# Graph network kernel: key one-hots as steps made by one Sign, counts from halved differences of neighbouring columns

## The reference

```python
x_j = x[src]
v_j = x_j[:, :384].reshape(E, 128, 3)
s_j = silu(x_j[:, 384:] @ W1 + b1) @ W3 + b3
edge_basis = rbf(edge_attr2) * cutoff @ W2 + b2
s1, s2, s3 = split(s_j * edge_basis)
v_msg = v_j * s1[:, :, None] + s3[:, :, None] * edge_attr1[:, None, :]
x = x + segment_sum(concat([v_msg, s2]), dst)
# second round: a message depends on the sender's node alone
msg2 = f(x, U, V, Wu1, Wu2)
x = x + segment_sum(msg2[src], dst)
out = layernorm(x_in + x)
```

## Time and profile before

| | |
|---|---|
| median of 3 runs | 541.85 us (537.26 to 544.62) |
| profiled execution | 537.99 us, of which the span is 536.1 us |
| PE busy | 461.1 us (86%), 5180 matmuls |
| DVE busy | 450.7 us (84%), 767 operations |
| ACT busy | 442.5 us (83%), 836 operations |
| POOL busy | 362.2 us (68%), 395 operations |

### The profile page before, as it was taken

The page is one execution under the profiler, slowest core; times in us unless marked ns, Lnnn a source line. Parts: engine busy times, 40 slices in busy tenths (PEclk is TensorE's granted clock), DMA queues, the critical chain, the costliest instruction groups (busy, mean ns, idle before and its releaser), DMA issues.

```text
span 536.1 us, 14464 instructions
## 1 busy us (share of the span) xinstructions
PE 461.1 (86%) x5180; PEld 291.1 (54%) x5181; DVE 450.7 (84%) x767; ACT 442.5 (83%) x836; POOL 362.2 (68%) x395
## 2 busy tenths in 40 slices
PE   4782989888997999997989899898899899789995
PEld 3321445455654655564655565565565566468784
DVE  4587899899999999999998999999999998641192
ACT  2362999888998999899899999999999999586442
POOL 8854777777777777777777777777777777370100
PEclk9765799899999999999999999999999999979999
DMA  8945888888888888888888888888888888410022
GB/s 230 334 157 153 251 263 261 261 274 269 261 246 280 258 273 272 258 253 268 264 254 262 284 264 261 270 269 260 238 259 266 279 274 263 153 45 1 2 99 98
DMA packets 46625, 123.17 MB, mean 230 GB/s; under 512 B 9379, under 2 KB 22249, under 8 KB 46545
## 3 DMA queue, kind: packets, MB, share of 16 engines
q0 software_dynamic: 25120, 102.91, 62.1%
q1 hardware_dynamic: 16993, 13.13, 7.9%
q10 hardware_dynamic: 4432, 6.10, 3.5%
HBM read 110.11 MB, written 12.00 MB: 228 GB/s over the span
## 4 chain that ended last, share of the span: by engine, by line
PE 29%; DVE 17%; POOL 17%; issue 13%; DMA 12%; ACT 11%; ACTq 1%; DVEq 1%; SPq 0%; POOLq 0%
POOL side L590 11%; PE psum L1512 8%; DMA side<-node_table,src_c 6%; DVE side L1091 5%; POOL work L590 5%; PE psum L1369 4%; PE psum L1407 4%; ACT side L714 4%; DMA xw<-in_x 3%; ACT scratch L723 3%; PE psum L1401 3%; PE psum L1381 2%; DVE side L1088 2%; DMA work<-node_table,src_c 2%; PE psum L1362 1%
## 5 line engine op out<-in xcount | busy, mean ns | idle before, releaser
L590 POOL DMA_INDIRECT side<-node_table,src_c x234 | 236.2, 1009 | 71.3 <-issue 67.7
L714 ACT ACTIVATE side<-key_no,less_key 128x320 bf16<-128x320 f32 x314 | 160.6, 567 | 0.4
L723 ACT ACTIVATE scratch<-side,one_f 128x640 bf16<-128x640 bf16 x157 | 129.6, 825 | 0.0
L1401 PE MATMUL psum<-side,scratch 128*32 128x512 f32 x468 | 124.0, 609 | 0.3 <-DVE side L1091 0.3
L1091 DVE TENSOR_TENSOR side<-side,psum 128x768 f32<-128x768 f32 x117 | 110.7, 946 | 0.0
L590 POOL DMA_INDIRECT work<-node_table,src_c x80 | 82.5, 1032 | 36.3 <-issue 34.5
L1369 PE MATMUL psum<-w2s,scratch 128*128 128x384 bf16 x314 | 79.2, 335 | 29.8 <-DVE side L1091 23.6
L1407 PE MATMUL psum<-side,scratch 128*32 128x128 f32 x1404 | 99.1, 277 | 0.0
L1088 DVE TENSOR_TENSOR side<-side,psum 128x512 f32<-128x512 f32 x117 | 79.6, 680 | 12.0 <-DMA side<-node_table,src_c 11.5
L1407 PEld LDWEIGHTS psum<-side,scratch 128*32 128x32 f32 x1404 | 71.6, 110 | 0.1
L1381 PE MATMUL psum<-scratch 128*128 128x320 bf16 x314 | 65.6, 318 | 0.0
(11 more groups left out here) (227 smaller groups left out, 772.1 us busy)
## 6 DMA issues: line engine op xcount, KB each, us to landing
side<-node_table,src_c POOLq DMA_INDIRECT x234
sum_rows<-stage SPq DMA_DIRECT2D x208, 16.0 KB
sum_rows<-zeros_bf SPq DMA_DIRECT2D x1, 2688.0 KB, 19.3
node_table<-work ACTq DMA_DIRECT2D x8, 320.0 KB, 2.9
scratch<-sum_rows SPq DMA_DIRECT2D x10, 256.0 KB, 4.6
out<-xw SPq DMA_DIRECT2D x9, 256.0 KB
xw<-in_x ACTq DMA_DIRECT2D x1, 1728.0 KB
work<-node_table,src_c POOLq DMA_INDIRECT x80
```

Of the source, the lines that this page charges most:

```text
L590: g.indirect_dma_start(out=rows[i % SLOT_PAIRS][:, j, :], out_offset=None, in_=node_table, in_offset=bass.IndirectOffsetOnAxis(ap=src_c[:, ...
L714: a.activation(key_off[:, b, j, :], key_no[:, :], ACT.Abs, bias=less_key[:, t:t + 1]).then_inc(L["key_off_made"], 1)
L723: a.activation(key_hot[:, n % 2, t:t + 2, :], key_off[:, b, :, :], ACT.Relu, bias=one_f[:, :], scale=-1.0).then_inc(L["key_hot_made"], 1)
L1401: mm(bank[b][j * SPAN:(j + 1) * SPAN, :], hot[:, n % 2, t + j, 0, :], rows[s][:, j, 0:4 * C], start=first, stop=True, skip_group_check=True)
```

## The change

The key one-hot of an edge becomes a step. `key_no` gets 33 columns a window in place of 32 (STEPS = SPAN + 1, KEYS = 330) and holds the column's key less one half. Sign(key_no + less_key) is -1 for columns up to the edge's key and +1 beyond it. One ACT operation a tile writes it straight into `key_hot`; the buffer `key_off` and its Relu go. PE multiplies as before, on 330 columns. Half the difference of two neighbouring columns of the product is the count of the one-hot. `add_counts` therefore takes two operations: `part_sum` = 0.5 x columns 1 to 32 + `counts`, then `counts` = -0.5 x columns 0 to 31 + `part_sum`, with a wait of DVE on its own first operation between. In the setup, the iota of `key_no` grows to 330 columns and its copy becomes a tensor_scalar.

```diff
-    KEYS = NW * SPAN
+    STEPS = SPAN + 1
+    KEYS = NW * STEPS
...
-        key_off = r_side.cut(4 * KEYS, BF16).rearrange("p (b j k) -> p b j k", b=2, j=2)
+        part_sum = r_side.cut(NW * SPAN).rearrange("p (s d) -> p s d", s=NW)
...
-            g.tensor_copy(key_no[:, :], key_no_i).then_inc(S["pool_const"], 1)
+            g.tensor_scalar(key_no[:, :], key_no_i, 0.5, None, ALU.add).then_inc(S["pool_const"], 1)
...
-            def key_offsets(i):
-                b = i % 2
-                if i >= 2:
-                    act.wait_ge(L["key_hot_made"], i - 1)
-                for j in range(2):
-                    t = 2 * i + j
-                    a.activation(key_off[:, b, j, :], key_no[:, :], ACT.Abs, bias=less_key[:, t:t + 1]
-                                 ).then_inc(L["key_off_made"], 1)
-
             def key_hots(i):
-                n, b = group_of(i), i % 2
+                n = group_of(i)
                 t = 2 * (i - GP * n)
-                act.wait_ge(L["key_off_made"], 2 * i + 2)
                 if n >= 2:
                     act.wait_ge(L["counted"], n - 1)
-                a.activation(key_hot[:, n % 2, t:t + 2, :], key_off[:, b, :, :], ACT.Relu, bias=one_f[:, :], scale=-1.0
-                             ).then_inc(L["key_hot_made"], 1)
+                for j in range(2):
+                    a.activation(key_hot[:, n % 2, t + j, :], key_no[:, :], ACT.Sign, bias=less_key[:, 2 * i + j:2 * i + j + 1]
+                                 ).then_inc(L["key_hot_made"], 1)
...
                 for i in range(PAIRS):
                     if i + GP < PAIRS:
-                        key_offsets(i + GP)
-                    if i + GP - 1 < PAIRS:
-                        key_hots(i + GP - 1)
+                        key_hots(i + GP)
...
-                v.tensor_tensor(into, into, bank[6][:, 0:KEYS].rearrange("p (s d) -> p s d", s=NW), ALU.add
-                                ).then_inc(L["counts_taken"], 1)
+                sums = bank[6][:, 0:KEYS].rearrange("p (s d) -> p s d", s=NW)
+                v.scalar_tensor_tensor(out=part_sum, in0=sums[:, :, 1:STEPS], scalar=0.5, in1=into, op0=ALU.mult, op1=ALU.add
+                                       ).then_inc(L["half_added"], 1)
+                dve.wait_ge(L["half_added"], n + 1)
+                v.scalar_tensor_tensor(out=into, in0=sums[:, :, 0:SPAN], scalar=-0.5, in1=part_sum, op0=ALU.mult, op1=ALU.add
+                                       ).then_inc(L["counts_taken"], 1)
...
-                pe.wait_ge(L["key_hot_made"], GP * n + tiles.stop // 2)
+                pe.wait_ge(L["key_hot_made"], 2 * GP * n + tiles.stop)
```

More of the change, by code:

```diff
@@ L37 @@
 MARGIN = 500
-SCRATCH = 20736
-SIDE = 9328
+SCRATCH = 20800
+SIDE = 9264
 HIGH_AT = 256
@@ L279, in build @@
         sums_in = [sem(f"sums_in{b}") for b in range(2)]
-        loop_names = """products_made basis_made src_hot_made key_off_made key_hot_made hot_made counted summed
+        loop_names = """products_made basis_made src_hot_made key_hot_made hot_made counted half_added summed
         copied combined sums_taken counts_taken table_step stored start_in angle_made turn_near turn_made sin_made wave_made
@@ L448, in _ @@
                     sp.wait_ge(L["src_hot_made"], LG)
-                    sp.wait_ge(L["key_off_made"], 2 * PAIRS)
-                    sp.wait_ge(L["key_hot_made"], PAIRS)
+                    sp.wait_ge(L["key_hot_made"], 2 * PAIRS)
+                    sp.wait_ge(L["half_added"], LG)
                     sp.wait_ge(L["hot_made"], 2 * LG)
@@ L534, in _ @@
             g.iota(lane_i, pattern=[[0, 1]], base=0, channel_multiplier=1).then_inc(S["pool_const"], 1)
-            g.iota(key_no_i.rearrange("p (s d) -> p s d", s=NW), pattern=[[KEY_STEP, NW], [1, SPAN]], base=0,
+            g.iota(key_no_i.rearrange("p (s d) -> p s d", s=NW), pattern=[[KEY_STEP, NW], [1, STEPS]], base=-1,
                    channel_multiplier=0).then_inc(S["pool_const"], 1)
@@ L788, in key_pass @@
                 for i in range(GP):
-                    key_offsets(i)
-                    if i:
-                        key_hots(i - 1)
+                    key_hots(i)
                 for i in range(PAIRS):
                     if i + GP < PAIRS:
-                        key_offsets(i + GP)
-                    if i + GP - 1 < PAIRS:
-                        key_hots(i + GP - 1)
+                        key_hots(i + GP)
                     if i % 2 and (i + 5) // 2 < QUADS:
@@ L1255, in _ @@
                 with dve.Fori(0, EXTRA) as r:
-                    dve.wait_ge(L["key_off_made"], 2 * PAIRS)
+                    dve.wait_ge(L["key_hot_made"], 2 * PAIRS)
                     dve.wait_ge(L["sums_taken"], LG)
```

## The result

The changed kernel takes 546.89 us in the median of four runs (545.35 to 550.14), the kernel before 539.56 us (535.91 to 544.62, four runs as well). The ratio is 1.0145 with a 95% interval of 1.0103 to 1.0187: slower, by more than nothing and by less than 2%. The profiled execution took 547.02 us with a span of 545.2 us, against 537.99 and 536.1 us. The forecast was 548 us.

A forecast was written before the change was run, and what follows sets the result against it. POOL's gathers were taken to pace the kernel, DVE next behind. DVE's 27.7 us of added work less 18.0 us of waits gave +9.7 us on the profiled 537.99 us: 548 us, range 542 to 555 us.

The forecast's parts named there:

- The pacer: In the pass, POOL's stream of gathers, 413 us, sets the pace, with DVE next behind at 95% busy.
- a round's 1.77 us less 0.95 us: ACT's one-hots: two Sign replace two Abs and a Relu, so ACT loses 0.8 us a pair, 129 us in 157 pairs.
- the later `key_hots`: In ACT's queue, `key_hots` of a new group runs later, behind `counted`, and still fits: cost 0.
- 1 to 3 us on the counts: On PE, 314 count matmuls grow from 320 to 330 columns: 1 to 3 us, hidden behind DVE, cost 0.
- The term a group: DVE's addition: two operations of 495 ns, the second waiting for the first, add 544 ns a group.
- by the rule: Between DVE's two additions, a semaphore costs nothing extra: a group would add 413 ns, giving +3.4 us, 541 us.
- rival B: DVE's second operation overlaps freely, or the usual execution leaves DVE more idle time: 541 to 544 us, chance 0.22.
- The waits: DVE's waits in the pass for gathered rows and ACT, 18.0 us together, vanish as DVE becomes late.
- rival C: DVE's waits move instead of vanishing, as later `counts_taken` holds PE's next count: 557 to 566 us, chance 0.18.
- Rival D: Faster: ACT was the real pacer and DVE's operations hide; gathers shrink, 518 us at best, chance 0.03.
- 27.7 - 18.0 = +9.7 us: In the pass, 27.7 us more DVE work less 18.0 us of filled DVE waits leaves +9.7 us.
- it moves as a whole: Behind the last message, the chain of last adds, copy, store and read of sums shifts without growing.

The follow-up runs named there:

- The kernel with ACT unrelieved: Kernel before with its two Abs and Relu kept on ACT, but two dependent halved additions on DVE: 547.41 us, ratio 1.0128.
- Both experiments without DVE's waits: Kernel before with only the two halved additions on DVE, 547.41 us; changed kernel with its first addition done twice, 564.74 us.
- DVE's part alone: Kernel before with Abs and Relu kept on ACT and the sums added in two dependent halves on DVE: 547.41 us, ratio 1.0128.
- the one with three additions: Changed kernel with the first addition done twice, the copy going to a spare buffer: 564.74 us, ratio 1.0459.

## Why the prediction was right, point by point

**The pacer.** I read POOL as the pacer and DVE as next behind. The swap fits: the stream of gathers measures 413.18 us before and 413.60 after. POOL issued as before, and it was DVE that ended 5.3 us later. That DVE had 18.4 us to spare before, and has none now, is measured. That POOL, and nothing else, set the pace before is read from its unbroken stream; no run on a 540 us chip changed the stream, or took work from DVE, to test it. The reading left out that POOL also waits 1.8 us for slots at `work`, in 6 waits, none over 0.3 us. It changes nothing.

**ACT.** Forecast busy 315 us, measured 337.2. The Sign costs what the Abs cost (566 ns at 330 columns, 567 at 320), which I had. The error is in the subtraction. I took a round's 1.77 us less 0.95 us, and both are times from start to start with the next operation right behind. A pair of Abs is busy for 1.01 us, so that 0.76 us is nearer. It lost 0.67 us a pair (105.3 us by 157) and not 0.8. I put the remaining 0.09 us down to overlap that ACT's operations lose now that it stands idle between them, which wasn't measured by itself. I also priced the later `key_hots` as fitting. It did: ACT's 87.7 us at L715 are a wait for `counted` with slack behind it, and DVE never waits for ACT in the pass.

**PE.** Forecast 1 to 3 us on the counts, hidden. The row grew from 65.6 to 67.3 us.

**DVE's two operations.** Forecast 495 ns each with 0.034 us between, measured 481 and 493 ns with 0.034 us. The term a group was +0.544 us and measured +0.524 (26.70 us by 51), mostly because the first operation is 14 ns cheaper. The 413 ns a group that the prediction gives "by the rule" don't follow from my own 495 ns, by which it is 2 x 413 - 398 = 428 ns, the upper end of rival B. That changes neither B's range nor its chance. The rival B fell with its first half, a second operation that overlaps, as the timeline at 144.38 shows, and so did its 541 to 544 us. Its second half, more idle time in the usual execution, comes up under the size.

**The waits.** Forecast -18.0 us, measured -18.4. This was rival C's point: waits could move instead of vanishing. None moved into DVE's pass. Rival D, a faster kernel, fell with it: DVE was the bound as soon as its waits were used up.

**The step that failed: "27.7 - 18.0 = +9.7 us".** The two terms were right to 1 us, but a third was missing. The other operations of DVE took 3.0 us less. In the pass before, 32 operations outside the dependent pairs started without overlapping their forerunner (26 behind idle gaps, 6 behind gaps that are too short to count as idle). After, there is 1. Each of these starts loses the 0.08 us of overlap besides its wait. 31 x 0.08 = 2.5 us, most of the 3.0. The kernel with ACT unrelieved has nearly the same saving with 4 such gaps left (its other operations take 369.3 us, the changed kernel's 368.8, those of before 371.8), so it comes from DVE being late and not from ACT.

**The other step that failed: "it moves as a whole".** The tail grew by 3.2 us. The first 0.8 us lie at PE. Its timeline around the end of the last message (start us, us, instruction), before and then after, and DVE's addition of the last group after:

```profile
464.37 1.04 PE L1381 MATMUL psum<-scratch 128*128 128x320 bf16 x6
465.75 0.62 PE L1401 MATMUL psum<-side,scratch 128*32 128x512 f32 x2 [0.34 <-DVE side L1091]
```

```profile
471.38 1.07 PE L1373 MATMUL psum<-scratch 128*128 128x330 bf16 x6
472.38 0.62 PE L1393 MATMUL psum<-side,scratch 128*32 128x512 f32 x2
```

```profile
470.61 0.95 DVE L1079 TENSOR_TENSOR side<-side,psum 128x768 f32<-128x768 f32 x1
472.59 0.49 DVE L1092 SCALAR_TENSOR_TENSOR side<-psum,work 128x320 f32<-128x320 f32 x1 [1.03 <-PE psum L1373]
...
482.97 1.08 DVE L1104 TENSOR_TENSOR scratch<-xw,scratch 128x384 f32<-128x384 f32 x1 [9.36 <-DMA scratch<-sum_rows]
```

The last six counts stand ahead of the last adds on PE. Before, PE was done with them and waited 0.34 us for the last message; after, they hold up the adds. From the end of the last message to the end of PE's last add of 128 columns 0.92 us passed before, 1.69 now. Both experiments without DVE's waits have it too (1.48 and 1.44 us). I read it as PE having less slack at the end when DVE no longer pauses, which was argued from the order and not tested by itself.

The other 2.4 us lie behind new_x1 (from its start to the end 59.85 us before, 62.24 after). PE in three stretches after (us, PE busy, granted clock, DMA share, GB/s), and then in three of before:

```profile
476.80:482.60 5.80, 5.72 (x24) 1.00 0.27 73
482.60:487.10 4.50, 1.10 (x5) 0.81 0.10 36
487.10:492.90 5.80, 5.77 (x18) 0.56 0.00 0
```

```profile
470.20:476.30 6.10, 6.05 (x14) 0.50 0.30 88
476.30:480.50 4.20, 3.10 (x15) 0.98 0.03 13
480.50:483.90 3.40, 3.40 (x18) 1.00 0.00 0
```

Between the last message and the last 5 us of the span each of the two executions has one stretch of 6.8 us at half of full clock, 1.2 of 2.4 GHz. Before, it lies at 470 us, while DVE waits for the stored sums and nothing hangs on PE. After, PE runs those matmuls at full clock, then has little to do until DVE's new_x1 is done, and the low clock falls on the matmuls that lead to the end. In the chain of work that ended last, the 12 matmuls of counts and updates that stand next took (start us, us), before and then after:

```profile
481.16 2.76 PE psum L1512 x12
```

```profile
488.25 4.65 PE psum L1504 x12
```

That is 1.9 us of the 2.4 in one piece. The kernel with DVE's part alone (59.79 us) and the one with three additions (60.16 us) don't pay it. So it isn't a consequence of two additions as such; where the low clock falls differs between programs, or between executions.

The traces show what PE did ahead of it. In the changed kernel the 24 matmuls of counts and updates in front of new_x1 run at full clock and are over at 482.6. PE then pauses:

```profile
485.41 1.09 PE L1414 MATMUL psum<-ident,scratch 128*128 128x128 f32 x4 [2.80 <-DVE scratch L1107]
```

The clock is at half from 485.4 to 492.2. Before, the first 14 of the 24 ran at half clock, they lasted until 478.9, and no pause behind them is over 1.1 us. The kernel without any addition has neither the Sign nor the two operations. Its profile, on a 630 us chip, has a pause of 2.81 us and 6.8 us at half clock as well, and 62.45 us from new_x1 to the end. Of the profiles with pauses of 1.1 to 1.4 us there, three have 59.7 to 60.2 us and five, with 3.4 us at half clock, 61.1 to 61.5. So in these profiles the longest tail goes with the long pause, and it came without this change too. Why the clock fell early in one execution and not in another stays open.

**The size.** Against the profiled execution the change cost 9.0 us, against the median 7.3. Four runs of before spread over 8.7 us and four of after over 4.8. I had argued that slower executions of before leave DVE more waits to fill. That is the second half of rival B, and 7.3 us lie between its 3 to 4 and the 9.7 of the forecast. The narrower spread fits it, but there is one trace of the kernel before, and no run was taken to test it. The forecast of 548 us was built on the profiled execution, which is 1.6 us under the median of before; built on the median it would have been 549.

## What to carry to other kernels

Before moving work from one engine to another, list the waits of the engine that receives it. What it adds is free up to the sum of those waits (18.4 us here, and 0.08 us more for each), and beyond that every start-to-start time counts in full: 0.40 us for each free operation of 320 columns, 0.51 us where the next one waits for it. Sparing an engine that the others hardly wait for (3.1 us here) buys next to nothing, though it is 83% busy: beside the two additions, 105 us fewer on ACT weren't worth anything that the times resolve. An independent operation between a dependent pair takes some 0.115 us off the engine; whether the kernel gains from it wasn't shown here.

## What the runs showed of the hardware

The same program, the kernel before, takes 536 to 545 us in some series and 618 to 635 us in others. On the chips of the latter PE's work is 10% longer in the pass (374.09 and 412.08 us for the same kernel) at a granted clock of 0.95 instead of 0.99, and its loads pause up to 2.9 us instead of 0.6 without a releaser that the profile shows. The clock alone explains some 4 points of those 10. The chains there also put 4 to 10% down to "another core or an unknown queue", which no page of a 540 us chip has. The cause of the rest and of the pauses stays open. With it the bound moves from DVE to PE, and a change that costs 4.6% on one chip costs 0.4% on the other.

On DVE an operation that waits for the one ahead starts 0.034 us behind its end, a free one 0.08 us before it, whether it reads PSUM or SBUF. SCALAR_TENSOR_TENSOR with a PSUM source takes 481 ns at 320 columns, where TENSOR_TENSOR takes 480.
